# Query projection, folding product and Newton steps reordered in the third layer; inverse square root in 8 operations instead of 11

## What is computed

```python
x = x + tanh(g_xattn[n]) * attention_n(layernorm(x), ctx, ...)
x = x + tanh(g_ffn[n]) * ffn_n(layernorm(x), ...)
```

```python
q = hidden @ q_proj_w.T ; k = cross @ k_proj_w.T ; v = cross @ v_proj_w.T   # split in heads
q = rmsnorm(q, q_norm_w) ; k = rmsnorm(k, k_norm_w)      # x * rsqrt(mean(x*x) + 1e-5) * w
scores = q @ k.T / sqrt(128) + attention_mask
out = (softmax(scores) @ v) @ o_proj_w.T
```

## Time and profile before

| | before |
|---|---|
| median of 3 executions | 2958.06 us (2956.93 to 2959.91) |
| the profiled execution's own time | 2956.89 us |
| its span in the profile | 2955.1 us |
| TensorE busy (matmul) | 2737.9 us, 93% |
| VectorE busy | 1799.1 us, 61% |
| ScalarE busy | 1048.9 us, 35% |
| GpSimd busy | 826.0 us, 28% |
| mean granted TensorE clock | 0.982 of full speed |

### The profile page before, as it was taken

The page is one execution under the profiler, slowest core; times in us unless marked ns, Lnnn a source line. Parts: engine busy times, 40 slices in busy tenths (PEclk is TensorE's granted clock), DMA queues, the critical chain, the costliest instruction groups (busy, mean ns, idle before and its releaser), DMA issues.

```text
span 2955.1 us, 45719 instructions
## 1 busy us (share of the span) xinstructions
PE 2737.9 (93%) x14480; PEld 2286.5 (77%) x14480; DVE 1799.1 (61%) x3749; ACT 1048.9 (35%) x2828; POOL 826.0 (28%) x707
## 2 busy tenths in 40 slices
PE   7987999999999998978888888889999999999998
PEld 5875888888888886767666666678878888888886
DVE  5766544644554556768888888855552555555557
ACT  3532333333333331234434333421123444444442
POOL 5011432432433242232222222235533222222200
PEclk8998999999999999989999999999999999999999
DMA  5010111110111110110000000011111000000000
GB/s 146 9 42 22 47 37 33 48 44 28 50 35 40 39 47 26 33 36 29 25 29 25 27 28 25 29 33 58 59 48 40 26 27 25 29 26 26 26 8 29
DMA packets 59816, 106.25 MB, mean 36 GB/s; under 512 B 7185, under 2 KB 11537, under 8 KB 59537
## 3 DMA queue, kind: packets, MB, share of 16 engines
q1 hardware_dynamic: 56448, 96.49, 11.3%
q10 hardware_dynamic: 3216, 7.81, 0.7%
HBM read 100.09 MB, written 2.10 MB: 35 GB/s over the span
## 4 chain that ended last, share of the span: by engine, by line
PE 81%; DVE 11%; issue 4%; ACT 3%; DMA 0%; DVEq 0%; POOL 0%; ACTq 0%; POOLq 0%
PE four L599 46%; PE outp L599 23%; PE value L599 7%; PE turned L945 3%; DVE nt L1549 2%; PE turned L721 1%; DVE nt L1551 1%; DVE sq L1731 1%; DVE x L1815 1%; DVE part L1735 1%; DVE a_lo L1915 1%; ACT a_hi L1217 1%; DVE stats L1577 1%; ACT qT L1217 1%; DVE xt_lo L1606 1%
## 5 line engine op out<-in xcount | busy, mean ns | idle before, releaser
L570 POOL TENSOR_TENSOR w_hi<-raw,zero 128x512 fp32r<-128x512 f32 x347 | 370.4, 1067 | 1977.1 <-PE four L599 693.4
L1815 DVE SCALAR_TENSOR_TENSOR x<-outp,g_inv,x 128x512 f32<-128x512 f32 x768 | 554.7, 748 | 400.9 <-PE outp L599 399.0
L574 POOL TENSOR_TENSOR w_lo<-raw,w_hi 128x512 fp32r<-128x512 f32 x352 | 453.9, 1290 | 32.0 <-ACT w_hi L1217 4.8
L599 PE MATMUL four<-xt_hi,w_lo 128*128 128x512 f32 x1024 | 425.8, 416 | 13.6 <-DVE xt_lo L1606 13.6
L599 PE MATMUL four<-xt_lo,w_hi 128*128 128x512 f32 x1024 | 407.3, 398 | 0.0
L599 PE MATMUL four<-xt_hi,w_hi 128*128 128x512 f32 x1024 | 407.1, 398 | 0.0
L599 PE MATMUL outp<-w_hi,a_lo 128*128 128x512 f32 x800 | 328.4, 411 | 62.2 <-DVE a_lo L1915 37.9
L1408 ACT ACTIVATE probs<-probs,top 128x128 f32<-128x128 f32 x512 | 199.6, 391 | 337.1 <-DVE top L1873 211.7
L599 PE MATMUL outp<-w_hi,a_hi 128*128 128x512 f32 x800 | 318.2, 398 | 0.0
L599 PE MATMUL outp<-w_lo,a_hi 128*128 128x512 f32 x800 | 316.4, 395 | 0.0
L1217 ACT ACTIVATE pT<-turned 128x512 f32<-128x512 f32 x320 | 191.3, 598 | 280.7 <-PE turned L945 222.8
(11 more groups left out here) (266 smaller groups left out, 4529.3 us busy)
## 6 DMA issues: line engine op xcount, KB each, us to landing
raw<-in_stream SPq DMA_DIRECT2D x352, 256.0 KB, 2.6
ctx_raw<-in_ctx_t ACTq DMA_DIRECT2D x4, 512.0 KB, 6.2
x<-in_x_in ACTq DMA_DIRECT2D x2, 1024.0 KB, 11.3
kz<-kT SPq DMA_DIRECT2D x32, 64.0 KB, 2.7
pb<-in_position_bias ACTq DMA_DIRECT2D x1, 2048.0 KB, 8.2
out<-x SPq DMA_DIRECT2D x8, 256.0 KB, 2.0
qw<-in_qweight ACTq DMA_DIRECT2D x1, 768.0 KB, 3.9
ln_w<-in_ln_weight ACTq DMA_DIRECT2D x1, 256.0 KB, 2.8
```

The costliest lines, as they stand in the source:

```text
L570: pool.tensor_tensor(w_hi[:, k, :], raw[:, k % RAW, :], zero[:, :].to_broadcast([P, D]), ALU.add)\
L574: pool.tensor_tensor(w_lo[:, k, :], raw[:, k % RAW, :], f32(w_hi[:, k, :]), ALU.subtract)\
L599: m = pe.matmul(out_, l, r, start=start, stop=stop, skip_group_check=True)
L1815: dve.scalar_tensor_tensor(out=x[:, b, :], in0=O[no_f(k) % 2][:, :], scalar=scale, in1=x[:, b, :], op0=ALU.mult, op1=ALU.add)\
```

## The change

1. In the third layer the query projection of a step has three parts (one, two and one quarters). The first quarter comes directly behind `turn`; output tiles 0 and 1 come behind it, ahead of the second part; tiles 2 and 3 ahead of the last.
2. The folding product of odd steps no longer comes first behind `turn` but behind output tiles 0 and 1.
3. `rsqrt_step` starts from another guess formula without the shift, makes one step of third order (five operations with its guess), and one Newton step (three operations), so 8 operations in place of 11, everywhere.
4. On VectorE the operations of `query_rstd` no longer lie among the scaling of the scores and ahead of the x additions; they begin behind the first x addition, three of them come ahead of tile 2, and the last two come behind `a_lo`.

```diff
--- before.py
+++ after.py
@@ -181,7 +181,7 @@
         if self.name == "L1":
             return [("q", t, 0, KT), ("k", t, 0, KT)]
         if self.name == "L2":
-            return [("q", 1 - t, 0, KT - 1), ("q", 1 - t, KT - 1, 1)]
+            return [("q", 1 - t, 0, 1), ("q", 1 - t, 1, KT - 2), ("q", 1 - t, KT - 1, 1)]
         return [("q", t // 2, t % 2 * 2, 2)]
 
     def made_head(self, i):
@@ -490,7 +490,7 @@
         HI_BY_ACT = range(2, 7)
         KEY_LAG = 3
         DENSE_AHEAD = 6
-        RSQRT = 11
+        RSQRT = 8
         LN2 = 2
 
 
@@ -998,11 +998,13 @@
                         early(n + 1, k - (L.NU - 1))
                     if 1 <= k <= L.NU:
                         turn(k - 1, it)
-                    if n == 2 and L.sums_head(k):
+                    if n == 2 and L.sums_head(k) and not L.parts(k):
                         q_squares(L.sums_head, k, it)
                     for no, (kind, hf, kt, kts) in enumerate(L.parts(k)):
-                        if n == 2 and L.has_O(k):
-                            output(k - L.lag_o, it, range(2 * no, 2 * no + 2))
+                        if n == 2 and no and L.has_O(k):
+                            output(k - L.lag_o, it, range(2 * no - 2, 2 * no))
+                        if no == 1 and n == 2 and L.sums_head(k):
+                            q_squares(L.sums_head, k, it)
                         def what_f(i, kind=kind, hf=hf):
                             return (kind, L.made_head(i), hf)
                         what = what_f(k)
@@ -1541,15 +1543,21 @@
             def rsqrt_step(j, v, y, t):
 
                 if j == 0:
-                    return dve.tensor_scalar(t.bitcast(I32), v.bitcast(I32), 1, None, ALU.logical_shift_right)
-                if j == 1:
-                    return dve.tensor_scalar(y.bitcast(I32), t.bitcast(I32), -1.0, float(0x5F3759DF),
+                    return dve.tensor_scalar(y.bitcast(I32), v.bitcast(I32), -0.5, float(0x5F3759DF),
                                              ALU.mult, ALU.add)
-                if j % 3 == 2:
+                if j in (1, 5):
                     return dve.tensor_tensor(t, y, y, ALU.mult)
-                if j % 3 == 0:
-                    return dve.scalar_tensor_tensor(out=t, in0=t, scalar=-0.5, in1=v, op0=ALU.mult, op1=ALU.mult)
-                return dve.scalar_tensor_tensor(out=y, in0=t, scalar=1.5, in1=y, op0=ALU.add, op1=ALU.mult)
+                if j == 2:
+                    return dve.tensor_tensor(t, t, v, ALU.mult)
+                if j == 3:
+                    return dve.scalar_tensor_tensor(out=t, in0=t, scalar=-10.0 / 3.0, in1=t,
+                                                    op0=ALU.add, op1=ALU.mult)
+                if j == 4:
+                    return dve.scalar_tensor_tensor(out=y, in0=t, scalar=5.0, in1=y, op0=ALU.add, op1=ALU.mult)
+                if j == 6:
+                    return dve.scalar_tensor_tensor(out=t, in0=t, scalar=-0.5 * 0.375 ** 3, in1=v,
+                                                    op0=ALU.mult, op1=ALU.mult)
+                return dve.scalar_tensor_tensor(out=y, in0=t, scalar=1.5 * 0.375, in1=y, op0=ALU.add, op1=ALU.mult)
 
             def rsqrt(v, y, t, sem_, base, final):
 
@@ -1867,18 +1875,15 @@
                                     in1=buf["madd"][:, :], op0=ALU.mult, op1=ALU.add)
                                 if j == 3:
                                     o.then_inc(s["seen"], 1)
-                                if j >= 2:
-                                    small(j - 2)
                             dve.wait_ge(s["seen"], at(L, lambda i: i + 1, k, it))
                             dve.tensor_reduce(top[:, k % 2, :], pr, AX_X, ALU.max, negate=True).then_inc(s["top"], 1)
                         else:
                             dve.tensor_reduce(top[:, k % 2, 0:rows], bank_, AX_X, ALU.max, negate=True)\
                                 .then_inc(s["top"], 1)
-                        small(2)
                     if n == 2 and k < L.NU and L.has_O(k):
-                        add_tiles(k, it, range(2), lambda j: small(3 + j))
+                        add_tiles(k, it, range(2), lambda j: small(j))
                     elif n == 2 and k < L.NU:
-                        small(3, 5)
+                        small(0, 2)
                     if 1 <= k <= L.NU:
                         scaled_gate(k - 1, it, small)
                     through(k, it, small)
@@ -1893,7 +1898,7 @@
                             .then_inc(s["sum"], 1)
                         dve.wait_ge(s["sum"], shift(lambda i: i + 1))
                     dve.reciprocal(inv[:, u % 2, 0:rows], sums[:, u % 2, 0:rows]).then_inc(s["inv"], 1)
-                    small(5, 7)
+                    small(2)
                     dve.wait_ge(s["inv"], shift(lambda i: i + 1))
                     dve.tensor_scalar(g_inv[:, u % 4, 0:rows], inv[:, u % 2, 0:rows], g, None, ALU.mult)\
                         .then_inc(s["g_inv"], 1)
@@ -1902,18 +1907,19 @@
 
                     if L.has_O(k):
                         if n == 2 and k < L.NU:
-                            add_tiles(k, it, range(2, B), lambda j: small(5 + j))
+                            small(3, 6)
+                            add_tiles(k, it, range(2, B), lambda j: small(4 + j))
                         else:
                             add_tiles(k, it)
                     elif n == 2 and k < L.NU:
-                        small(7, 9)
-                    small(9, STEPS)
+                        small(3, 8)
                     if L.has_V(k):
 
                         dve.wait_ge(s["a_hi"], at(L, lambda i: i - L.lag_v + 1, k, it))
                         w = L.nb * P
                         dve.tensor_tensor(buf["a_lo"][:, 0:w], V[:, 0:w], f32(buf["a_hi"][:, 0:w]),
                                           ALU.subtract).then_inc(s["a_lo"], 1)
+                    small(8, STEPS)
                     if n == 2 and L.pieces(k):
                         query_turn(lambda i: L.pieces(i)[0], k, it)
                     tail_stats(k)
```

## The result

The change takes the kernel from 2957.7 us to **2884.1 us** (medians of four runs each; ratio 0.975, 95% interval 0.973 to 0.977).

The account below looks back on a forecast made before the run. In the third layer's attention TensorE and VectorE, both near 83% busy, wait for each other in turn. Pairs 40.9, entry and exit 2, inverse square root elsewhere 5: 48 us off, so 2910, range 2893 to 2935.

Parts of the forecast that it names:

- the turns: Third layer's loop: six turns add 21 us, with a VectorE gap of 2.6 us each that the change leaves.
- The pair, 17.6: Third layer's attention: each of 29 pairs of steps gains 1.41 us, 17.6 in place of 19.03, 40.9 in all.
- Folding product later: Odd step on TensorE: the 1.66 us wait for `part` goes; with the first quarter ahead, 1.37 us gained.
- First quarter ahead: Query projection on TensorE: covers the odd step's wait with the later fold; free in the even step.
- 8 operations: Inverse square root on VectorE: three operations saved at 0.20 us each, 0.6 us a pair.
- Newton behind the x additions: VectorE, third layer: `a_lo` starts 1.68 us earlier, with 0.27 lost afterwards to two operations put behind it.
- Rival 1: Third layer: small operations miss the GpSimd splits, up to 0.35 us more a pair, clock some 4; 2896; chance 0.13.
- Rival 2: Third layer: more small operations are caught by splits, losing about 1 us a pair; 2939; chance 0.08.
- Rival 3: Third layer: only the removed operations count, 0.6 us a pair; 2934; chance 0.08.
- rival 4: Third layer: the quarter ahead of the output tiles delays x additions 0.69 us a step; slower, 2979; chance 0.04.
- Rival 5: Third layer: first quarter held for its bank, gains cancel, time within 0.2% of now; no gain, chance 0.05.
- Elsewhere: Other norms and key rows: 5 us from saved operations (1.2, 1.2, 2.6), nothing where TensorE has early products.

Follow-up runs that it names:

- e6: Kernel before with 8 operations and the folding product behind output tiles 0 and 1, query quarter not moved, VectorE's order as before: 2871.3 us, ratio 0.969.
- e1: Kernel before with the 8-operation inverse square root alone, both orders of work as before: 2904.0 us, ratio 0.982.
- e7: Kernel before with 8 operations and the first query quarter ahead of the output products, folding product still ahead of both: 2905.2 us, ratio 0.982.
- e5: Kernel before with TensorE's two moves and the 8 operations, without the new order on VectorE: 2873.6 us, ratio 0.971.
- e10: The change with the query projection back in its place, folding product behind tiles 0 and 1, VectorE's new order and 8 operations kept: 2884.7 us, ratio 0.976.
- e2: The change with the old 11-operation inverse square root, everything else kept: 2944.7 us, ratio 0.996.
- e4: Kernel before with TensorE's two moves alone, VectorE and the 11 operations as before: 2932.2 us, ratio 0.991.
- e9: Kernel before with 256 memsets on VectorE ahead of the second layer's loop, so later code lies 256 instructions later: 2959.5 us, ratio 1.001.
- e3: Kernel before with 64 memsets on VectorE ahead of the second layer's loop, so the third layer's loop lies 64 instructions later: 2940.6 us, ratio 0.995.
- e8: The change with 64 memsets on VectorE ahead of the second layer's loop, so the third layer's loop lies 64 instructions later: 2907.8 us, ratio 0.982.

## Why the prediction was wrong

**The step that failed is the turns.** The prediction put it as "a gap of VectorE with no releaser, 2.6 us each, which the change leaves as it is", and forecast 20.3 to 22 us over a turn, where 17.92 were measured. The view had no releaser to show, and the step took that for a fixed price of turning the loop. It is a fetch of instructions: gap and packets come and go together in every run (33 or 34 packets in the 29 pairs with the gap, 4 without). Over all runs a turn costs 0.1 to 0.2 us more than a plain pair where VectorE's code lies well and 2.6 to 5.4 where it lies badly, and that depends on how many instructions stand in the loop and anywhere ahead of it. The three operations saved in each inverse square root shorten the loop and all code ahead of it, and this moved it into a good place: 20.1 us. The view of the DMA queues carried the hint, 34 packets of instruction fetches in this stretch, and the prediction didn't read it. Without this term the change would have come to 2904, inside the range, and that in part by luck: the pairs gave 4.4 us less than forecast, the other layers and the key rows 7.6 more, and 4.4 came from a clock that is not the change's.

**The pair, 17.6: nearly right in size, wrong in its split.** Measured 17.77, so the pairs gave 36.5 us and not 40.9. The walk held at most points: tile 2 of the odd step at 5.53 (forecast 5.45), the next scores at 8.67 (8.43), `a_lo` at 9.91 (9.77), the even step's x addition at 13.97 (13.74), its tile 2 at 14.77 (14.54). Two small operations are caught by the splits, as forecast, and VectorE doesn't wait for `outp` in the odd step. The lost 0.2 us lies between tile 2 and the scores: 3.14 us against the 2.98 of the earlier trace rows, where tile 2 had not waited. The even step's wait of tile 2 is 0.92, where over 1 us was forecast.

The runs take the sum apart otherwise than the prediction did.

1. *Folding product later*: the forecast of 1.37 in the odd step counted it with the quarter. e6 against e1 shows 1.01 for it alone.
2. *First quarter ahead*: forecast as free in the even step and as half of the gain in the odd one. It gives 0.00 (e7 against e1), costs 0.07 (e5 against e6) and gives 0.06 (e10 against the change). It was never needed: the two output tiles cover the wait for `part` by themselves.
3. *8 operations*: 0.70 a pair, 0.23 for each one saved. The forecast took 0.6 for the pair from the spacing of 0.20; besides, one operation no longer meets a split. e1's timeline of VectorE, where before had 0.63 and 1.14:

```profile
1588.37 0.63 DVE L1556 SCALAR_TENSOR_TENSOR nt<-nt 128x8 f32<-128x8 f32 x1
1589.04 0.17 DVE L1558 SCALAR_TENSOR_TENSOR rq<-nt,rq 128x8 f32<-128x8 f32 x1
1589.99 0.69 DVE L1921 TENSOR_TENSOR a_lo<-value,a_hi 128x512 fp32r<-128x512 f32 x1 [0.78 <-ACT a_hi L1217]
```

The small operations are now done before `a_hi` is there (`a_lo` waits 0.78 us for it), so at this place fewer of them would probably bring nothing more; no run tried it.

The price that the prediction took from the Trainium skill was only a part of what the page says. The section "The TRN2 errata" of "VectorE: DVE Perf Modes" also says that its row of 58 cycles falls short, and puts a `tensor_tensor` add of float32 at 151 cycles and one per element at 0.96 GHz, measured there at 512 and 2048 elements: an estimate of 0.17 us for 8. The trace agrees (0.15 to 0.17 for an operation that meets no split), so page and trace don't differ as the prediction had it.

4. *Newton behind the x additions*: forecast as a gain. It costs 0.31 with 11 operations (e2 against e4; there five small operations and not two stand behind `a_lo`), 0.38 (the change against e5) and 0.51 (e10 against e6) with 8. In the old order one small operation is held by a split in a pair; in the new one two are, the second right ahead of `a_lo`. Two more now stand between `a_lo` and `part`: 1.70 us from one to the other (1613.01 to 1614.71), where e6 has 1.35. Both delays lie ahead of the x additions of the even step, for which TensorE waits 0.92. That the two make up the whole cost is argued; the runs moved them only together. The prediction priced this at 0.27 and thought that the operations taken from the front would pay for it. They don't, since in e6 they lie in gaps between 512-wide operations, and tile 2 doesn't wait for them.

**The rivals.** None came about as told. Rival 1 has the nearest time (2896), but its cause, no operation caught, is not there; its clock term, 4 us, was a piece of the true cause (three turns of before at the lower clock, 1.4 us each above the other three). Rival 2 would need pairs of 18.6. Rival 3 is excluded by e4, which gains 0.98 a pair without removing an operation, rival 4 by e5 and e7. Rival 5 had the gains cancel, which they didn't.

**Elsewhere: 18 us and not 5, or 7 with the entry and exit.** Here a second step of the prediction was too small: it put the other norms and key pairs at nothing, since TensorE has early products to do there. Second layer's attention: 861.2 us, against 864.9 before; e1 and e5 have 861.1 and 861.2, e2, e3 and e4 864.9 to 865.0 (e9, whose 256 memsets lie there, 867.6). So this is the 8 operations, 3.7 where 1.2 was forecast. TensorE's waits for this layer's `probs` fall by 1.6 us; where the other 2.1 lie is open. The stretch with the key rows: 124.8, e1 125.1; with 8 operations at most 127.6 (e6), with 11 at least 132.2 (e9). This is them too, 7.8 where 2.6 was forecast: TensorE's waits for the key rows' `probs` fall from 7.4 us in all to 1.4, and 3.5 of these 6.0 are at the one place where the wait was 4.20 and is 0.74. The end gives 1.1, as forecast (1.2).

The fourth layer's 4.4 us are not the change's. Its first 162 us, before, after, and e9, which is the kernel before with its code at the same place modulo 256:

```profile
2188.10:2350.00 161.90, 157.32 (x799) 132.27 (x799) 64.53 (x145) 59.40 (x147) 37.73 (x33) 0.98 0.12 36
```

```profile
2118.60:2280.50 161.90, 157.44 (x818) 132.85 (x818) 66.12 (x145) 61.36 (x153) 37.78 (x34) 1.00 0.12 36
```

```profile
2192.20:2354.10 161.90, 157.38 (x816) 132.49 (x815) 66.30 (x148) 61.36 (x153) 37.68 (x33) 1.00 0.13 36
```

In the same time more is done where the granted clock is 1.00 and not 0.98. Between the two landmarks around it, before's execution takes 727.6 us, e9's 723.1, the change's 723.2. The other runs come out both ways too, with 11 operations (e2 723.0, e4 727.4) and with 8 (e10 722.5, e5 727.7), and what lowers the clock in some executions stays open.

**The sum again, from what was measured**: 36.5 (pairs) + 20.1 (turns) + 3.7 + 7.8 (8 operations elsewhere) + 1.1 (end) + 1.7 (exit) + 4.4 (clock, not the change) - 0.7 (start) = 74.6 of 75.1 us.

## What to carry to other kernels

An idle row whose releaser is "issue", once for each turn of a loop, is a question about where the code lies: look at the queue of instruction fetches in the same window, and shift the code by a few dozen instructions ahead of the loop before anything in the loop is tuned. Time each part of a compound change by itself: here one of the two moves on TensorE gave all that they gave, the other gave nothing, and the new order on VectorE took 11 us back or more (0.38 x 29), so that e6, the later fold with 8 operations alone, beats the whole change by 13 us (0.969 against 0.975 of before). A small operation that stands in a gap between large ones costs nothing that could be seen here; moved out of there to "where there is time", it can land against another engine's access or ahead of the operation that everyone waits for.

## What the runs showed of the hardware that was not expected

The same VectorE loop costs 0.2 us at a turn or 2.7 and more, by its place alone. A shift of 64 instructions takes the gap away (e3) or brings it (e8), one of 256 leaves it (e9). In the bad place 33 or 34 packets of instruction fetches run in the 29 pairs, in the good one 4.

With the gap often comes a second price, TensorE's clock. Two turns of the kernel before by stretch, the cheapest and the dearest, from pick to pick (columns as in the earlier trace rows):

```profile
1391.65:1413.37 21.72, 16.52 (x92) 13.62 (x91) 16.37 (x42) 8.65 (x25) 4.64 (x4) 1.00 0.08 28
1628.35:1651.73 23.38, 18.11 (x92) 15.02 (x91) 16.42 (x43) 8.73 (x25) 4.64 (x4) 0.93 0.10 33
```

With the clock at 1.00 a bad turn stands 2.6 to 2.9 us above a plain pair (three of before, three of e4, two of e9). With 0.92 or 0.93 it is 4.0 to 4.4 (three of before, two of e4, five of e8, four of e9), with 0.85 it is 4.9 to 5.4 (six of e2, one each of e4 and e8). In the turn shown above the stretch at 1.2 GHz comes behind the gap. No turn without a gap has a dip, but some plain pairs do (e7). Why e2 and e8 have a dip at all six turns, e9 at four and before and e4 at three is open.
